# Thirteen steps instead of fourteen at the end of a second attention, with late additions moved up, and two matrix products in place of eight for bias columns

## The reference

```
x = x + cross_attention(layernorm(x), ctx)         # 16 heads, 1601 keys, a mask, out @ w_o.T
x = x + self_attention(layernorm(x))               # 16 heads of 32, over the 64 rows of a batch
x = x + mixture(layernorm(x))                      # 20 experts, the best 2 for each token

# self_attention, for the 16 heads of each batch:
qkv = x @ w_qkv + b_qkv
q = q + (q @ a_q) @ b_q * 2 ;  v = v + (v @ a_v) @ b_v * 2
out = softmax(q @ k.T * 32**-0.5) @ v
return out @ w_proj + b_proj

# mixture, for each token:
h = gelu(x @ wg1 + bg1) ;  probs = softmax(h @ wg2 + bg2)
y = sum over the top 2 of probs: prob * (x @ We[e] + be[e])
```

## Time and profile before

| What | Value |
|---|---|
| Median of three runs | 773.29 us (771.12 to 774.63) |
| The profiled execution | its span is 772.6 us, and that is the time which the profile gives for it |
| TensorE (PE) busy | 708.0 us, 92% |
| VectorE (DVE) busy | 410.2 us, 53% |
| ScalarE (ACT) busy | 360.6 us, 47% |
| GpSimd (POOL) busy | 289.0 us, 37% |

### The profile page before, as it was taken

How to read it: one execution, slowest core, us unless ns; L and a number is a source line. 1 busy time by engine, 2 the same in 40 slices (tenths; PEclk the granted TensorE clock), 3 DMA queues, 4 the chain that set the end, 5 groups by cost and what they waited for, 6 DMA issues and landing times.

```text
span 772.6 us, 16928 instructions
## 1 busy us (share of the span) xinstructions
PE 708.0 (92%) x6817; PEld 581.6 (75%) x6817; DVE 410.2 (53%) x938; ACT 360.6 (47%) x665; POOL 289.0 (37%) x259
## 2 busy tenths in 40 slices
PE   1999999999999999999999999999999766999970
PEld 0787788778878887888788977887778554788860
DVE  5834434453344424533543345735368348799965
ACT  2425445453545345535454343533455431599950
POOL 0005135513553255225532453432225132788530
PEclk9999999999999999999999999999999985799995
DMA  8401101220021101110110002021001580999818
GB/s 294 149 1 43 45 2 45 98 91 24 29 98 44 44 2 44 44 39 7 44 44 2 3 3 75 1 79 45 3 29 57 188 303 21 330 394 397 333 52 326
DMA packets 30268, 74.77 MB, mean 97 GB/s; under 512 B 4053, under 2 KB 4437, under 8 KB 29155
## 3 DMA queue, kind: packets, MB, share of 16 engines
q1 hardware_dynamic: 25778, 65.16, 23.6%
q0 software_dynamic: 4400, 8.41, 2.9%
HBM read 66.13 MB, written 13.44 MB: 103 GB/s over the span
## 4 chain that ended last, share of the span: by engine, by line
PE 86%; DVE 6%; DMA 3%; ACT 2%; issue 2%; SPq 0%; POOL 0%; DVEq 0%; POOLq 0%; ACTq 0%
PE bank L188 22%; PE bank L190 21%; PE bank L189 20%; PE bank L194 10%; PE bank L345 4%; PE bank L322 3%; DMA raw<-in_wq 2%; DVE x_sb L1611 1%; PE bank L564 1%; DMA wr<-scratch_ys 1%; PE bank L551 1%; PE bank L665 1%; PE bank L580 1%; DVE wh L1084 1%; DVE stats L1340 0%
## 5 line engine op out<-in xcount | busy, mean ns | idle before, releaser
L1637 POOL TENSOR_SCALAR pp<-pp,rl 128x400 f32<-128x400 f32 x128 | 163.8, 1297 | 234.8 <-DVE rl L1162 234.8
L1217 DVE COPY pt<-bank 128x512 f32<-128x512 f32 x64 | 44.3, 692 | 99.4 <-PE bank L194 99.3
L188 PE MATMUL bank<-chi,wk 128*128 128x400 f32 x256 | 93.5, 365 | 0.0
L844 ACT ACTIVATE pp<-pp,acc 128x400 f32<-128x400 f32 x128 | 79.0, 619 | 28.0 <-DVE acc L1250 27.7
L1250 DVE CUSTOM_DVE_ANT_0 pp<-bank,cap 128x400 f32<-128x400 f32 x128 | 66.8, 569 | 46.5 <-PE bank L322 46.5
L190 PE MATMUL bank<-chi,wk 128*128 128x400 f32 x256 | 88.3, 345 | 0.0
L189 PE MATMUL bank<-clo,wk 128*128 128x400 f32 x256 | 88.3, 345 | 0.0
L188 PE MATMUL bank<-wv,chi 128*128 128x512 f32 x200 | 83.5, 417 | 0.0
L189 PE MATMUL bank<-wv,chi 128*128 128x512 f32 x200 | 78.5, 393 | 0.0
L190 PE MATMUL bank<-wv,clo 128*128 128x512 f32 x200 | 78.5, 392 | 0.0
L761 ACT ACTIVATE pt<-bank 128x512 f32<-128x512 f32 x64 | 38.2, 597 | 76.4 <-PE bank L194 75.3
(11 more groups left out here) (238 smaller groups left out, 1387.4 us busy)
## 6 DMA issues: line engine op xcount, KB each, us to landing
wr<-in_We SPq DMA_DIRECT2D x13, 1024.0 KB, 11.6
craw<-in_ctx SPq DMA_DIRECT2D x16, 800.0 KB, 4.4
raw<-in_We SPq DMA_DIRECT2D x8, 1024.0 KB, 10.5
acc<-in_We SPq DMA_DIRECT2D x6, 1024.0 KB, 11.0
scratch_xn<-acc SPq DMA_DIRECT2D x16, 256.0 KB
wr<-scratch_ys SPq DMA_DIRECT2D x8, 512.0 KB, 7.2
x_sb<-in_x SPq DMA_DIRECT2D x2, 1024.0 KB, 8.5
out_dram<-x_sb SPq DMA_DIRECT2D x8, 256.0 KB, 5.9
```

Of the source, the lines that this page charges most:

```text
L188: pe.matmul(o, lhs[0], rhs[0], start=start, stop=False)
L844: act.activation(frame(p8), frame(p8), ACT.Exp, bias=bias, scale=-1.0, accum_out=total).then_inc(S["a_exp"], 1)
L1217: dve.tensor_copy(pt[:, p8 % 4, :, :].rearrange("p a c -> p (a c)"), at("t", 8 * (n - 1) + p8)[:, :]).then_inc(S["v_pt"], 1)
L1637: pool.tensor_scalar(frame(p8), frame(p8), rl[:, n % 2, p8:p8 + 1], None, ALU.mult).then_inc(S["g_pn"], 1)
```

## The change

The list `beside` is one entry shorter from step 9 on. The projection of tile 6 goes behind the values of tile 7 in step 9, ahead of the turn of tile 4. The projection of tile 7 goes into step 10, followed by the turns of tiles 5 and 6. The first gate product stands at the start of step 11.

DVE makes the additions of tiles 4 and 5 in step 9 (tile 5 without a step between), ahead of the low part of tile 7 (line 1457), and the addition of tile 6 behind it; the addition of tile 7 comes in step 10. The addition and its statistics are now a function, `add_projection`.

ACT makes the norms of tiles 4 and 5 in step 9 behind line 1020 and ahead of the high part of turned tile 4, the norm of tile 6 behind that part, and the norm of tile 7 in step 10 behind the high parts of turned tiles 5 and 6. The activation that loads the Gelu table moves from step 9 to the end of step 8.

POOL makes the factors of tiles 4, 5 and 6 in step 9 and those of tile 7 in step 10. The row stores and weight loads on the DMA queues keep their order.

The eight products of one column at lines 514 to 516 become two of four columns, on the same weights.

```diff
-            for c in range(8):
-                last = pe.matmul(pb[6][:, c:c + 1], mbd[:, c // 4, :], bcol[:, c + c // 4 * 4:c + c // 4 * 4 + 1],
-                                 start=True, stop=True)
+            for j in range(2):
+                last = pe.matmul(pb[6][:, 4 * j:4 * j + 4], mbd[:, j, :], bcol[:, 8 * j:8 * j + 4], start=True, stop=True)
...
-                  ([("v2", 7)], [], [("pj", 4), ("n2", 3)]), ([("pj", 5)], [], [("n2", 4)]),
-                  ([("pj", 6)], [], [("n2", 5)]), ([("pj", 7)], [], [("g1", 0), ("n2", 6), ("ga", 1)]),
-                  ([], [], [("n2", 7)]), ([], [], [("g1", 1)])]
+                  ([("v2", 7)], [], [("pj", 4), ("n2", 3)]), ([("pj", 5)], [], [("pj", 6), ("n2", 4)]),
+                  ([("pj", 7)], [], [("n2", 5), ("n2", 6)]), ([("g1", 0)], [], [("n2", 7), ("ga", 1)]),
+                  ([], [], [("g1", 1)])]
...
-        add_at = {i: step_of["pj", i] + (i < 7) for i in range(8)}
-        norm_at = {i: step_of["pj", i] + 1 for i in range(8)}
+        add_at = {i: step_of["pj", i] + (i < 5) for i in range(6)}
+        add_at[7] = step_of["pj", 7]
+        late_add_at = {6: step_of["pj", 6]}
+        norm_at = {i: step_of["pj", i] + 1 for i in range(4)}
+        late_norms = {9: ([4, 5], [6]), 10: ([], [7])}
...
-                if step >= 8:
+                if step == 8:
                     norms(step)
-                if step == 9:
-                    act.activation(warm[:, :], gw[:, 20:21], ACT.Gelu)
-                if step == 12:
-                    gelu(0)
                 if 0 <= step - 2 < 8:
...
                 if step < 8:
                     norms(step)
+                before_turns, behind_turns = late_norms.get(step, ([], []))
+                for i in before_turns:
+                    norm(8 + i, i, xall[:, i, :])
                 beside_read(beside[step][2])
+                for i in behind_turns:
+                    norm(8 + i, i, xall[:, i, :])
+                if step == 8:
+                    act.activation(warm[:, :], gw[:, 20:21], ACT.Gelu)
+                if step == 11:
+                    gelu(0)
...
+            def add_projection(i):
+                dve.wait_ge(S["g_xb"], i + 1)
+                dve.wait_ge(S["p_pj"], i + 1)
+                dve.tensor_tensor(x_sb[:, i, :], x_sb[:, i, :], pb[bank_of("pj", i)][:, :],
+                                  ALU.add).then_inc(S["v_x2"], 1)
+                dve.wait_ge(S["v_x2"], i + 1)
+                stat(i)
...
-                for i in range(8):
+                for i in add_at:
                     if add_at[i] == step:
...
+                        add_projection(i)
...
                     ins.then_inc(S["v_h2"], 1)
+                for i in late_add_at:
+                    if late_add_at[i] == step:
+                        add_projection(i)
                 norm2_lo(beside[step][2])
...
-                    if add_at[j] == i:
+                    if i in (add_at.get(j), late_add_at.get(j)):
                         factors(8 + j, j)
```

More of the change, by code:

```diff
@@ L986, in norms @@
             def norms(step):
-                for i in range(8):
+                for i in range(4):
                     if norm_at[i] == step:
```

## The result

The kernel after took 764.03 us (median of four runs, 762.74 to 766.29) against 773.96 us before: ratio 0.987, 95% interval 0.9848 to 0.9892. A second comparison, later, gave 763.55 against 774.04 us, ratio 0.9857, 0.9839 to 0.9874. The forecast was 762.4 us with a range of 760.0 to 766.5. The profiled span fell from 772.6 to 762.3 us, 10.3 us; 10.9 were forecast.

A forecast was written before the change was run, and what follows sets the result against it. TensorE was taken as the bound (86% of the chain of waits), losing time to idleness and low clock. End 9.5 plus bias 1.4 gives 10.9 us off the 773.3 us median: 762.4 us, range 760.0 to 766.5.

The forecast's parts named there:

- The end: End of the attention: TensorE's idle brackets and low clock go, 9.5 us gained, logits at 621.9 against 631.41.
- Its clock: End of the attention: 2.7 us of the gain from the 1.2 GHz level behind almost 4 us of idleness.
- Rival B: End of the attention gives less, 6 to 8 us, clock loss being of one execution: 765.8 us, chance 0.18.
- The table load: Gelu table load on ACT, moved ahead of the wait for tile 7's values: 1.4 us, cost nothing.
- the 1.38 us weighed in the prediction: Drain the Trainium skill adds to a table load, about 2.66 us per switch; cover would shrink to 0.1 us.
- POOL: POOL's factor operations beside DVE's low parts that read a bank: 0.55 us each, cost zero.
- The alternative price: POOL's factors at 0.94 us, as beside SBUF-only DVE work: 0.39 us for each of tiles 6 and 7, 0.8 in all.
- The stores: Wait for all stores ahead of line 1545: costs at most 1.2 us, taken as zero, stores released some 9 us earlier.
- The bias products: Front: four matmuls in 0.5 us and no clock fall behind them; 1.4 us gained, bounds -0.3 and +1.4.
- the pauses of 1.2 and 1.3 us: TensorE pauses left in the new front; a clock fall there costs the product behind up to 1.7 us.
- Its bound: Front: second turn waits for DVE's low parts of turned tiles 0 and 1, starting at 488.25 instead of 489.6.
- The rule on the clock: Clock falls after idle time; by that alone the old kernel keeps its clock and the bias edit brings nothing.

The follow-up runs named there:

- bias alone: Kernel before with only the two four-column bias products: 773.33 us, ratio to before 0.9986.
- end alone: Kernel after with the old one-column bias products put back: 765.96 us, ratio to before 0.990.
- The removal: Kernel after with the old bias products and without the activation that loads the Gelu table early: 767.01 us.
- the longer POOL operation: Kernel after with the old bias products and one more POOL operation of 0.63 us ahead of the factors of tiles 6 and 7: 766.86 us, run once.
- the last kernel: Kernel after with split logits, reordered front, and high parts of turned tiles 4 and 5 ahead of the norm of tile 7: 761.01 us, ratio to before 0.9829.
- the kernel with split logits alone: Kernel after with the logits of the first four tiles made as soon as the first Gelu is there: 762.05 us.
- the front reordered too: Split logits, plus high and low parts of turned tiles 0 to 3 made earlier on ACT and DVE, ahead of norms and additions: 764.16 us.

## Why the prediction was right, point by point

**The end.** Forecast from the start of tile 5's projection to the logits 18.3 us, and in both kernels that projection starts 2.95 us ahead of the values of tile 7: 18.35 us measured. The steps hold one by one, shifted by the 0.2 us at which this stretch starts later: norms of tiles 5, 6 and 7 forecast at 609.7, 613.2 and 616.4, found at 609.90, 613.47 and 616.68; last turn at 617.3, found at 617.63.

**Its clock.** 2.7 us of the 9.5 were the low clock behind the 3.9 us of idleness. It was there in the profile read, and a second profile of that order (bias alone) lost 1.1 us less. Rival B named this. It put the end at 6 to 8 us; the profiles give 8.4 and 9.5, and the timed end alone 8.0 with an interval from 5.3 to 10.1, so the runs do not exclude it.

**The table load.** Free, as forecast. It began 0.02 us behind the activation ahead of it, and the next one began 0.01 us behind its end, so nothing like the 1.38 us weighed in the prediction came on top. The removal shows that it would be free in a second place too.

**POOL.** Its operation took 0.55 us beside the new neighbours; the zero was right. The alternative price was not: 0.39 us for each of two tiles was summed to 0.8, and the longer POOL operation shows that such delays lie beside each other. It should have been 0.4.

**The stores.** They did not show on the path. In the kernel after, the DMA engines are busy until about 634, and line 1558, behind the wait, starts at 635.44 without an idle bracket:

```profile
630.00:633.00 3.00, 1.83 (x6) 1.35 (x6) 2.44 (x12) 0.44 (x2) 0.67 (x2) 0.50 0.95 369
633.00:635.00 2.00, 1.11 (x5) 0.71 (x8) 1.82 (x6) 0.92 (x3) 0.30 (x1) 0.50 0.16 60
```

That is one to two microseconds of slack. In the kernel before they had been idle from 635 on the earlier trace rows, so the traffic ended only about one microsecond earlier. The last store was issued 6.74 us earlier and not some 9, because SP was still issuing the row stores ahead of it (8.73 us for eight, from 614.37 on). SP's last store and the weight load behind it, first before, then after:

```profile
629.88 0.28 SPq L1876 DMA_DIRECT2D scratch_xn<-xi  x1
630.29 0.38 SPq L1851 DMA_DIRECT2D raw<-in_We  x1
```

```profile
623.14 0.35 SPq L1889 DMA_DIRECT2D scratch_xn<-xi  x1
623.62 0.38 SPq L1864 DMA_DIRECT2D raw<-in_We  x1
```

As this load of 1 MB follows the last store in both, the end of the traffic is not the landing of the stores, which no row shows. "I take zero" came true, but its reason, stores released 9 us earlier, was too strong.

**The bias products.** The mechanism stands and the size is off as a mean. In the profile read the front gained 1.27 us of the 1.35 forecast. But the prediction said itself that without the fall of the clock the gain is nothing, and the fall happens in only three of six executions with the old products. The mean over those six is (9.84 + 9.81 + 9.82 + 8.57 + 8.58 + 8.56)/6 - 8.57 = 0.63 us, and the timed runs of this edit alone gave 0.7 us with an interval that holds zero. So the term of 1.4 should have been 0.6. On top of the end's edit the medians give 1.9 us (9.9 against 8.0), but the interval of the 8.0 is too wide to tell the two apart. Of the pauses of 1.2 and 1.3 us that the prediction names in the new front, only one of 1.29 us is there; besides it stand the 0.71 us ahead of the bias products, as before, and 0.2 us by which the eight matmuls of the two turns take longer than the usual 1.03.

**Its bound.** The reason given, that DVE's and ACT's chain and not TensorE decides when the turn of tile 2 starts, is shown by the last kernel: with that chain reordered the front took 6.88 us, with the same matmuls.

**The rule on the clock** from the Trainium skill (TensorE: Matmul & The Clock Gate, Part 1), that idle time lets it fall, would have left the clock up here. In three of six executions it fell behind 0.71 to 0.74 us of idleness and 1.92 us of one-column matmuls that the windows count as busy, so by itself that rule does not tell this case. The same page of the Trainium skill says that what watches the engine's activity runs freely and does not start anew with a kernel. That the same instructions at the same distances end either way here fits that.

**What the number owes to luck.** The forecast was 1.6 us too low, and only part of that is in its sum. It took a gain read from one profile off the median of three other runs. In every run for which both are known the time is 1.76 to 1.91 us above the span, so by my estimate the profile of 772.6 us stands for a time of 774.4 us, 1.1 above the 773.29 it was set against. The later medians of the kernel before, 773.96, 774.0 and 774.04, are 0.7 us above that number too. With the bias term at 0.6 and the end at the mean of the two profiles (0.5 less), the sum is 9.6 instead of 10.9 us. Off 774.0 the recorded sum gives 763.1 and the corrected one 764.4 us; the measured 763.55 and 764.03 lie between, so the times do not say which is better.

## What to carry to other kernels

When the last tiles go around several in-order engines, write down for each engine what is ready when, and put every instruction that waits for a late product behind all that is ready: here one addition on the wrong side of one DVE group cost 4.5 us, and one norm 1.5 us. Take the clock that follows an idle stretch as a range and not as the number of the one trace, and delays of chains that do not feed each other as a maximum and not as a sum. Set a gain read from a profile against that profile's own time, not against the median of other runs. A reorder that frees one wait can bring up the next ten microseconds later, so read the timeline past the place of the edit.

## What the runs showed of the hardware

Two executions differ by some microseconds at places that no edit here touches. The bias products began between 482.85 and 484.43 us. TensorE's first matmul starts at 16.03 us in the kernel before and at 16.88 in the kernel after, which is 0.85 of the 1.42 us in the first row of the account. Behind the logits lay between 140.2 and 143.6 us. Part of that is the clock: the expert blocks begin at the low level, and it rose 6.2 us after their start in the kernel before (660.1 to about 666.3) but 4.3 us after it in the kernel after (650.84 to about 655.1), which by half is 0.9 us. From the first to the last matmul of the blocks it took 88.34 and 87.47 us; that is 0.87 of the 1.03 us in the last row of the account. Windows, first before, then after:

```profile
660.00:666.00 6.00, 5.89 (x16) 0.50 0.99 348
```

```profile
650.00:655.00 5.00, 4.35 (x11) 0.50 0.97 344
655.00:656.00 1.00, 1.00 (x8) 0.93 1.01 375
```

The rest lay in two places. One is inside the blocks: they took 87.38 us in the kernel with split logits alone and 90.24 with the front reordered too, where TensorE had two waits that the other did not have:

```profile
664.09 0.47 PE L188 MATMUL bank<-wh,xu 128*128 128x512 f32 x1 [1.11 <-issue]
668.30 0.47 PE L188 MATMUL bank<-xu 128*128 128x512 f32 x1 [0.77 <-ACT xm L765]
```

The other is behind the last matmul, in the load of the results and the last additions: 23.76 us in the kernel before, 25.67 in the one with the end alone. Why those waits come and why that load takes longer in some executions stays open.
